# Masking the diagonal score chunks on TensorE instead of VectorE in the maximum pass of a two-pass attention kernel

## The chip, the cores and the metric

The kernel runs on one core of a Trainium2 chip. The metric is the device time of one execution in microseconds; the kernel before takes 3775.22 us (median of three runs, 3775.03 to 3777.12). TensorE (PE, with its weight loads shown apart as PEld), VectorE (DVE), ScalarE (ACT), GpSimd (POOL) and the DMA queues each have their own instruction stream, and they meet through counting semaphores.

## The reference

Input x is 2 x 2048 x 1024 in float32. One layer of causal attention with 32 query heads of 32 columns, one shared key head and one shared value head, and a bias linear in the distance; then a feed-forward layer whose low-rank part is chosen per token; a layer norm behind each. Cut to what matters here:

```python
q = (x @ Wq).reshape(b, s, 32, 32)
k, v = split(x @ Wkv)                     # one head of 32 columns each
scores = einsum('bqhd,bkd->bhqk', q, k) * scale + slopes * (kpos - qpos)
scores = where(kpos <= qpos, scores, -inf)
out = softmax(scores) @ v                 # -> @ Wo, + x, layer norm
# then: x @ W.T + b + routed low-rank part, + x, layer norm
```

## The kernel before

The attention takes the first 2870 us or so of the execution, the feed-forward part the rest; the change is in the attention alone.

**Units.** A unit `g` is one segment of 512 queries (4 tiles of 128) with 4 of the 32 heads: 2 batches x 4 segments x 8 head groups = 64 units. Segment `s` (0 to 3) of a batch sees `s + 1` segments of keys. A query's keys are handled twice: a maximum pass finds each row's largest score ahead of time, and a main pass computes the exponentials with that maximum already folded in.

**The maximum pass (step A).** For each head `h`, query tile `t` and key segment `c` there is one chunk: `scores_for_max` (L697 on) multiplies a query tile (97 rows, stationary) with 512 keys (moving) into one of three PSUM banks `ps_a` (L707), and `maximum` (L580 on) on VectorE takes the largest of each row into one column of `mxp`. In the key segment that holds the queries themselves (`c == s`), only `(t + 1) * 128` columns are needed (128, 256, 384 or 512), and the last 128 of these are a triangle that has to be masked. These masked chunks are 16 of each unit, 1024 in all; the other 1536 chunks are 512 wide and need no mask. VectorE handles an unmasked chunk with one `tensor_reduce` (L587), a masked one with `tensor_tensor_reduce` (L590), which adds the mask `maska` to the bank and takes the maximum, and which shows in the profile as two instructions: the custom operation, and a read of its accumulator into `mxp`. Before L590 VectorE's queue also holds a semaphore increment (`went_on`) that nobody waits for.

**Banks.** TensorE waits before each chunk for `a_done` of the chunk three before it (`count - 2`). VectorE waits for `a_full` of its own chunk. The transposes of x (step X) and of the maxima (step T) go through the same three banks and counters.

**The main pass (step S).** For each key tile `k` and head `h` TensorE computes scores of 128 keys by up to 512 queries into one of two banks `ps_s` (L774), adds a triangular mask on the diagonal with a second matmul of `identb` and `maskt` in bf16 (L777), and ScalarE takes the exponential into `prob` (L507). S waits for the exponential two before it (`e_done`), so no more than two score tiles stand ahead. Then `over_keys` (L719) multiplies `prob` with the values into `ps_o` and with ones into `ps_sum`: four heads side by side, each with 32 columns of weights. Each such call shows as 8 matmuls in the trace.

**What sets the order.** `plan_unit` lays steps out over the slots of a unit by tables of slot numbers: beside the S steps of unit `g` stand the A chunks of units `g + 1` and `g + 2`, the projection of the queries of unit `g + 2` (Q, L673 to L675), the transposes of x and the inversions of the row sums. All engines walk the same plan, each doing its own part, in order.

Of the kernel before, what the change touches and what calls it, by code (L numbers as in the profile page):

```python
# [6 lines left out]
ALU = mybir.AluOpType  # L7
ACT = mybir.ActivationFunctionType
AX = mybir.AxisListType
F32 = mybir.dt.float32  # L10
F32R = mybir.dt.float32r
BF16 = mybir.dt.bfloat16
I32 = mybir.dt.int32

P = 128
# [5 lines left out]
QB = 512  # L21
NSEG = T // QB
QT = QB // P
SCALE = DH ** -0.5
EPS = 1e-5
MASKED = -1.0e30
START = 1
PROBS = 6
KR = 3 * DH + 1
# [17 lines left out]
def seg_of(g):  # L47

    return g // HG
# [7 lines left out]
def full_tiles(g):  # L57

    return ktiles(g) - QT


def steps_before(g):
    return sum(ktiles(x) for x in range(g))
# [15 lines left out]
def ring(sg):  # L79

    return sg % RING * QB
# [7 lines left out]
def bank_of(count):  # L89
    return count % 3  # L90


def slot_of(count):
    return count % PROBS
# [96 lines left out]
def program(nc, x, wq, wkv, wo, w, bias, la, lb, gate_w, gate_b, out):  # L191
    nc.disable_value_cache = True
    slopes = alibi_slopes(NH)
    att = nc.dram_tensor("att_scratch", (UNITS, QT, P, P), F32, kind="Internal").ap()
    slope_rows = nc.dram_tensor("slope_rows", (NH, QB), F32, kind="Internal").ap()

    xb = x.rearrange("b (s t p) d -> (b s) p t d", t=QT, p=P)
    xt = x.rearrange("b (i p) d -> (b i) p d", p=P)
    ot = out.rearrange("b (i p) d -> (b i) p d", p=P)
    wq_v = wq.rearrange("(c p) (g m) -> g p c m", p=P, m=P)  # L200
    wo_v = wo.rearrange("(c p) n -> c p n", p=P)
    w_v = w.rearrange("(o p) n -> o p n", p=P)

    with ExitStack() as ctx:
        def sem(name):
            return ctx.enter_context(nc.semaphore(name))

        def sb(c, name, shape, dt):
            return c.enter_context(nc.sbuf_tensor(name, shape, dt))

        def pb(c, name, shape, dt=F32):
            return c.enter_context(nc.psum_tensor(name, shape, dt))

        ident = sb(ctx, "ident", [P, P], F32)
        attention(nc, sb, pb, sem, slopes, xb, wq_v, wkv, att, slope_rows, ident)
        feed_forward(nc, sb, pb, sem, xt, ot, wo_v, w_v, bias, la, lb, gate_w, gate_b, att, ident)


def attention(nc, sb, pb, sem, slopes, xb, wq_v, wkv, att, slope_rows, ident):
    with ExitStack() as ctx:  # L220
        identb = sb(ctx, "identb", [P, P], BF16)
        maska = sb(ctx, "maska", [P, QB], F32)
        maskt = sb(ctx, "maskt", [P, P], BF16)
        ones = sb(ctx, "ones", [P, DH], F32)
        slope = sb(ctx, "slope", [P, NH], F32)
# [7 lines left out]
        base = sb(ctx, "base", [GH * QT, SEGS, HG], F32)  # L233
# [11 lines left out]
        kmax = sb(ctx, "kmax", [P, RING * QB], F32R)  # L245
# [5 lines left out]
        mxp = sb(ctx, "mxp", [P, GH * QT, NSEG], F32)  # L251
# [10 lines left out]
        ps_a = [pb(ctx, f"ps_a{i}", [P, QB]) for i in range(3)]  # L262
# [6 lines left out]
        def counter(name):  # L269

            counters.append(sem(name))
            return counters[-1]

        pool_c = sem("pool_c")
# [4 lines left out]
        went_on = sem("went_on")  # L279
# [28 lines left out]
        a_done = counter("a_done")  # L308
# [5 lines left out]
        def units(prologue, unit_step, epilogue):  # L314

            prologue()  # L320
            count = FIRST
            for g in range(UNITS):
                plan = plan_unit(g)
                unit_step(g, plan, count)
                count += sum(what in ("A", "CT", "X") for what, _ in plan)
            epilogue(count)
# [3 lines left out]
        with nc.Block() as start:  # L330
            @start.sync
            def _(sp):
                for c in counters:
                    sp.sem_inc(c, START)
# [71 lines left out]
        @block.gpsimd  # L406
        def _(pool):
            nc.gpsimd.memset(ident[:], 0.0).then_inc(pool_c, 1)
            nc.gpsimd.memset(identb[:], 0.0).then_inc(pool_c, 1)
            nc.gpsimd.memset(maska[:], 0.0).then_inc(pool_c, 1)  # L410
            nc.gpsimd.memset(maskt[:], 0.0).then_inc(pool_c, 1)
            nc.gpsimd.memset(ones[:], 1.0).then_inc(pool_c, 1)
            nc.gpsimd.iota(dist_i[:], [[P, DIST0 + QT]], base=-P * DIST0, channel_multiplier=1).then_inc(pool_c, 1)
            pool.wait_ge(pool_c, 6)
            nc.gpsimd.iota(kpos_i[3 * DH:KR], [[1, QB]], base=0, channel_multiplier=0).then_inc(pool_c, 1)
            pool.wait_ge(pool_c, 7)
            for m in (ident, identb):
                nc.gpsimd.affine_select(out=m[:], in_=m[:], compare_op=ALU.not_equal, fill=1.0, base=0,
                                        pattern=[[-1, P]], channel_multiplier=1).then_inc(pool_c, 1)
            nc.gpsimd.affine_select(out=maska[:, QB - P:], in_=maska[:, QB - P:], compare_op=ALU.is_ge, fill=MASKED, base=0,  # L420
                                    pattern=[[-1, P]], channel_multiplier=1).then_inc(pool_c, 1)
            nc.gpsimd.affine_select(out=maskt[:], in_=maskt[:], compare_op=ALU.is_ge, fill=MASKED, base=0,
                                    pattern=[[1, P]], channel_multiplier=-1).then_inc(pool_c, 1)

            def split_wq(number):
                pool.wait_ge(wqh_done, START + number + 1)
                nc.gpsimd.tensor_tensor(wql[:], wq_raw[:], wqh[:].bitcast(F32), ALU.subtract).then_inc(wql_done, 1)  # L427

            def divide(g):

                pool.wait_ge(r_done, START + QT * (g + 1))
                pool.wait_ge(at_out, START + 16 * g)
                nc.gpsimd.tensor_tensor(at_sb[:], o_sb[:], r_sb[:], ALU.mult).then_inc(at_done, 1)

            def prologue():
                for number in range(3):
                    split_wq(number)

            def step(g, plan, count):
                steps = steps_before(g)  # L440
                for what, arg in plan:
                    if what == "WS":
                        split_wq(g + 3)
                    if what == "R" and arg == QT:
                        divide(g - 1)
                    if what == "ADD":
                        k = 2 * arg
                        c1 = max(0, k + 1 - full_tiles(g)) * P
                        even, odd = (prob[slot_of(steps + k + i)] for i in range(2))
                        pool.wait_ge(e_done, START + GH * (steps + k + 2))  # L450
                        pool.wait_ge(pv_done, START + steps + k + 1)
                        nc.gpsimd.tensor_tensor(even[:, :, c1:], even[:, :, c1:], odd[:, :, c1:],  # L452
                                                ALU.add).then_inc(pair_done, 1)

            units(prologue, step, lambda count: divide(UNITS - 1))
# [63 lines left out]
        def _(dve):  # L519
# [22 lines left out]
            for r in range(3):  # L542
                cols = slice(r * DH, (r + 1) * DH)
# [36 lines left out]
            def maximum(count, g, i, chunk):  # L580
                h, t, c, cols = chunk
                if i == 0:
                    dve.wait_ge(c_max, START + g)
                ps, top = ps_a[bank_of(count)][:, 0:cols], mxp[:, h * QT + t, c:c + 1]
                dve.wait_ge(a_full, START + count + 1)
                if c < seg_of(g) % NSEG:
                    nc.vector.tensor_reduce(top, ps, AX.X, ALU.max).then_inc(a_done, 1)  # L587
                else:
                    dve.sem_inc(went_on, 1)
                    nc.vector.tensor_tensor_reduce(ps, ps, maska[:, QB - cols:], 1.0, MASKED, ALU.add, ALU.max,  # L590
                                                   top).then_inc(a_done, 1)

            def reduce_max(g, count):
                s = seg_of(g) % NSEG
# [57 lines left out]
        def _(pe):  # L652
# [4 lines left out]
            for u in range(HG):  # L657
                last = nc.tensor.matmul(ps_m[0:GH * QT, P + u:P + u + 1],
                                        slope4[:, u * GH:(u + 1) * GH].rearrange("p h t -> p (h t)"),
                                        ident[:, 0:1], start=True, stop=True)  # L660
# [39 lines left out]
            def scores_for_max(count, g, i, chunk):  # L700
                h, t, c, cols = chunk
                sg = seg_of(g) // NSEG * NSEG + c
                ps, buf = ps_a[bank_of(count)], g % 3
                if i == 0:
                    pe.wait_ge(stack_in, START + 32 * (g + 1))
                pe.wait_ge(a_done, START + max(0, count - 2))
                last = nc.tensor.matmul(ps[:, 0:cols], qst[buf][0:KR, h, t * P:(t + 1) * P],  # L707
                                        kmax[0:KR, ring(sg):ring(sg) + cols], start=True, stop=True)
                last.then_inc(a_full, 1)

            def turn_max(g, count):
# [521 lines left out]
```

## Time and profile before

| | |
|---|---|
| median of three runs | 3775.22 us |
| the profiled execution | 3775.03 us |
| its span, first to last instruction | 3773.2 us |
| mean granted TensorE clock | 0.984 of full |
| busy: PE / PEld | 3582.0 us (95%) / 2207.2 us (58%) |
| busy: DVE / ACT / POOL | 2415.6 us (64%) / 1927.6 us (51%) / 1358.9 us (36%) |
| unmasked chunks on DVE (L587) | 1536, 682 ns each |
| masked chunks on DVE (L590) | 1024, 503 ns each, and 1024 accumulator reads, 130 ns each |

Matmuls are pipelined: a matmul's recorded duration is longer than the time until the next one starts, so the time that one takes on TensorE is read from start to start. A weight load (PEld) belongs to the matmul behind it and runs beside the matmul before it. A number in square brackets at the end of a row is the idle time of the engine ahead of that row and what ended it.

### The profile page before, as it was taken

The page shows a single profiled execution, that of the slowest core. Times are in us where ns is not written, and L with a number is a line of the kernel's source. Part 1 is how long each engine was busy: PE and PEld are TensorE (multiplying, and loading weights), DVE is VectorE, ACT ScalarE, POOL GpSimd, SP SyncE. Part 2 cuts the span into 40 slices and gives each one's busy share as a digit, 9 for nine tenths or more (in the row PEclk, how much of TensorE's full clock was granted, in tenths as well). Part 3 has the DMA queues.
Part 4 walks back from the last instruction along what each step waited for, and adds up shares of the span by engine and source line. Part 5 has one row for each costly group of instructions (what it writes and reads, how often), then busy time and mean ns, then how long its engine had stood idle before and what let it go on. Part 6 is the DMA issues. An engine that isn't in the chain of part 4 may idle for free. (4 is left out here: it accounts for less than half of the span.)

```text
span 3773.2 us, 56666 instructions
## 1 busy us (share of the span) xinstructions
PE 3582.0 (95%) x21057; PEld 2207.2 (58%) x21057; DVE 2415.6 (64%) x5438; ACT 1927.6 (51%) x3252; POOL 1358.9 (36%) x419
## 2 busy tenths in 40 slices
PE   5899999999999999899999999999995999999998
PEld 4555554455444444555554455544432888989987
DVE  4777777777776763777777777777742444444444
ACT  2656656666676756656666666676764101001000
POOL 1114444544455544124445554454552011011010
PEclk8999999999999999999999999999997999999999
DMA  2121110010000011111110000000003121121221
GB/s 85 46 60 32 49 32 24 24 38 23 21 15 21 15 35 32 49 57 32 49 32 24 24 15 23 21 15 21 10 7 123 45 67 55 62 67 50 67 67 40
DMA packets 157358, 148.11 MB, mean 39 GB/s; under 512 B 8356, under 2 KB 140452, under 8 KB 155016
## 3 DMA queue, kind: packets, MB, share of 16 engines
q1 hardware_dynamic: 157128, 145.07, 13.1%
q8 instruction: 140, 2.29, 0.3%
q14 instruction: 90, 0.74, 0.1%
HBM read 94.13 MB, written 33.62 MB: 34 GB/s over the span
## 5 line engine op out<-in xcount | busy, mean ns | idle before, releaser
L507 ACT ACTIVATE prob<-ps_s,alibi 128x512 f32<-128x512 f32 (+3 forms) x2560 | 1525.5, 623 | 868.6 <-PE ps_s L777 435.7
L452 POOL TENSOR_TENSOR prob<-prob 128x2048 f32<-128x2048 f32 (+1 forms) x240 | 1046.8, 4362 | 1091.4 <-ACT prob L507 1091.4
L587 DVE TENSOR_REDUCE mxp<-ps_a 128x1 f32<-128x512 f32 x1536 | 984.1, 682 | 384.4 <-PE ps_a L707 376.1
L774 PE MATMUL ps_s<-qst,kexp 97*128 97x512 f32 (+3 forms) x2560 | 1047.9, 417 | 42.5 <-ACT prob L507 28.4
L707 PE MATMUL ps_a<-kmax,qst 97*128 97x512 f32 (+3 forms) x2560 | 961.9, 396 | 38.8 <-DVE mxp L590 23.1
L774 PEld LDWEIGHTS ps_s<-qst,kexp 97*128 97x128 f32 x2560 | 481.6, 189 | 788.5 <-ACT prob L507 613.5
L719 PE MATMUL ps_o<-prob,val 128*32 128x512 f32 (+3 forms) x5120 | 602.1, 542 | 6.0 <-ACT prob L507 6.0
L590 DVE CUSTOM_DVE_ANT_0 ps_a<-ps_a,maska 128x128 f32<-128x128 f32 (+3 forms) x1024 | 495.4, 503 | 163.0 <-PE ps_a L707 130.1
L707 PEld LDWEIGHTS ps_a<-kmax,qst 97*128 97x128 f32 x2560 | 489.3, 194 | 113.4 <-DVE mxp L590 47.2
L972 POOL TENSOR_TENSOR hb_sb<-h_sb,bias_b 128x1024 f32<-128x1024 f32 x32 | 76.8, 2401 | 792.7 <-DVE z_sb L1116 732.4
L719 PE MATMUL ps_sum<-prob,ones 128*32 128x512 f32 (+3 forms) x3200 | 347.0, 513 | 0.0
L610 DVE RECIPROCAL r_sb<-s_sb 128x128 f32<-128x128 f32 x256 | 240.9, 944 | 133.0 <-ACT s_sb L513 133.0
L1002 ACT ACTIVATE root<-var 128x1 f32<-128x1 f32 x64 | 13.0, 203 | 606.5 <-DVE var L1061 606.5
L427 POOL TENSOR_TENSOR wql<-wq_raw,wqh 128x1024 fp32r<-128x1024 f32 x64 | 152.0, 2375 | 330.5 <-ACT wqh L466 330.5
L1173 PE MATMUL ps_z<-wth,hth 128*128 128x364 f32 x768 | 254.9, 332 | 5.3 <-DVE htl L1128 5.3
L1175 PE MATMUL ps_z<-wtl,hth 128*128 128x364 f32 x768 | 252.9, 329 | 0.0
L1177 PE MATMUL ps_z<-wth,htl 128*128 128x364 f32 x768 | 252.8, 329 | 0.0
L777 PE MATMUL ps_s<-maskt,identb 128*128 128x128 bf16 x1024 | 237.1, 233 | 0.0
L576 DVE SCALAR_TENSOR_TENSOR qst<-ps_m,qst 32x512 fp32r<-32x512 f32 x256 | 176.1, 688 | 80.8 <-ACT qst L473 75.6
L1165 PE MATMUL ps_y<-woh,ath 128*128 128x512 f32 x512 | 206.9, 404 | 3.9 <-DVE atl L1049 3.9
L719 PEld LDWEIGHTS ps_o<-prob,val 128*32 128x32 f32 x5120 | 105.7, 108 | 175.1 <-issue 152.5
L673 PE MATMUL ps_m<-xh,wqh 128*128 128x512 f32 x512 | 205.4, 401 | 0.4 <-DVE val L570 0.4
(147 smaller groups left out, 3673.7 us busy)
## 6 DMA issues: line engine op xcount, KB each, us to landing
wq_raw<-in_L_attn_Wq SPq DMA_DIRECT2D x64, 512.0 KB, 3.9
xs<-in_L_attn_hidden_states SPq DMA_DIRECT2D x8, 2048.0 KB, 8.1
qst<-qst SPq DMA_DIRECT2D x64, 256.0 KB
att_scratch<-at_sb SPq DMA_DIRECT2D x64, 256.0 KB, 2.4
at_raw<-att_scratch SPq DMA_DIRECT2D x32, 512.0 KB, 5.2
x_sb<-in_L_attn_hidden_states SPq DMA_DIRECT2D x32, 512.0 KB, 4.2
out<-z_sb SPq DMA_DIRECT2D x32, 512.0 KB, 3.1
z_sb<-in_L_attn_Wo SPq DMA_DIRECT2D x4, 512.0 KB, 5.4
```

What stands on the lines that cost most here:

```text
L452: nc.gpsimd.tensor_tensor(even[:, :, c1:], even[:, :, c1:], odd[:, :, c1:], ALU.add).then_inc(pair_done, 1)
L507: nc.scalar.activation(prob[slot_of(steps + k)][:, h, c0:], ps_s[h % 2][:, c0:], ACT.Exp, bias=alibi_of(g, h, k - full_tiles(g))).then_inc ...
L587: nc.vector.tensor_reduce(top, ps, AX.X, ALU.max).then_inc(a_done, 1)
L590: nc.vector.tensor_tensor_reduce(ps, ps, maska[:, QB - cols:], 1.0, MASKED, ALU.add, ALU.max, top).then_inc(a_done, 1)
L610: nc.vector.reciprocal(r_sb[:, cols], s_sb[:, cols]).then_inc(r_done, 1)
L707: last = nc.tensor.matmul(ps[:, 0:cols], qst[buf][0:KR, h, t * P:(t + 1) * P], kmax[0:KR, ring(sg):ring(sg) + cols], start=True, stop=True)
L719: last = nc.tensor.matmul(ps[h * DH:(h + 1) * DH, c0:], weights, prob[slot_of(steps_before(g) + k)][:, h, c0:], start=k == 0, stop=k == kt ...
L774: last = nc.tensor.matmul(bank[:, c0:], kexp[0:KR, at:at + P], qst[g % 3][0:KR, h, c0:], start=True, stop=not diagonal)
L777: last = nc.tensor.matmul(bank[:, c0:c0 + P], identb[:], maskt[:], start=False, stop=True)
L1173: nc.tensor.matmul(ps, hth[:, c], wth[:, c, piece(p)], start=c == 0, stop=False, skip_group_check=True)
L1175: nc.tensor.matmul(ps, hth[:, c], wtl[:, c, piece(p)], start=False, stop=False, skip_group_check=True)
L1177: last = nc.tensor.matmul(ps, htl[:, c], wth[:, c, piece(p)], start=False, stop=False, skip_group_check=True)
```

## The change

The mask goes from VectorE to TensorE, in the way that the main pass already has it. `scores_for_max` follows a masked chunk's matmul by a second one, which adds a triangle of -1e30 (`maskb`, bf16, 128 x 128) to the last 128 columns of the bank, with `identb` as its stationary operand; only this one raises `a_full`. VectorE uses the same `tensor_reduce` for every chunk, now also with 128, 256 and 384 columns; the custom operation, its accumulator read and the `went_on` increment are gone. The mask tile is smaller: 128 x 128 in bf16 instead of 128 x 512 in float32.

```diff
-        maska = sb(ctx, "maska", [P, QB], F32)
+        maskb = sb(ctx, "maskb", [P, P], BF16)
...
                 dve.wait_ge(a_full, START + count + 1)
-                if c < seg_of(g) % NSEG:
-                    nc.vector.tensor_reduce(top, ps, AX.X, ALU.max).then_inc(a_done, 1)
-                else:
-                    dve.sem_inc(went_on, 1)
-                    nc.vector.tensor_tensor_reduce(ps, ps, maska[:, QB - cols:], 1.0, MASKED, ALU.add, ALU.max,
-                                                   top).then_inc(a_done, 1)
+                nc.vector.tensor_reduce(mxp[:, h * QT + t, c:c + 1], ps_a[bank_of(count)][:, 0:cols], AX.X,
+                                        ALU.max).then_inc(a_done, 1)
...
                 last = nc.tensor.matmul(ps[:, 0:cols], qst[buf][0:KR, h, t * P:(t + 1) * P],
-                                        kmax[0:KR, ring(sg):ring(sg) + cols], start=True, stop=True)
+                                        kmax[0:KR, ring(sg):ring(sg) + cols], start=True, stop=sg < seg_of(g))
+                if sg == seg_of(g):
+                    last = nc.tensor.matmul(ps[:, cols - P:cols], identb[:], maskb[:], start=False, stop=True)
                 last.then_inc(a_full, 1)
```

On TensorE, in a unit of segment 2, one round of the four heads with masked chunks between the S steps and the products with the values. Before (`ps_a` with a number is one of the three banks, `kmax` the keys, `qst` the queries; `prob,val` are the products with the values):

```order
L774 MATMUL ps_s1<-qst1,kexp 128x512
L707 MATMUL ps_a1<-kmax,qst2 128x128
L719 MATMUL ps_o<-prob1,val 32x512 x4
L774 MATMUL ps_s0<-qst1,kexp 128x512
L707 MATMUL ps_a2<-kmax,qst2 128x256
L774 MATMUL ps_s1<-qst1,kexp 128x512
L707 MATMUL ps_a0<-kmax,qst2 128x384
L774 MATMUL ps_s0<-qst1,kexp 128x512
L707 MATMUL ps_a1<-kmax,qst2 128x512
L774 MATMUL ps_s1<-qst1,kexp 128x512
```

The same place in the changed kernel, whose lines have other numbers (L771 is S, L702 the chunk, L705 the new matmul, L716 the products):

```order
L771 MATMUL ps_s1<-qst1,kexp 128x512
L702 MATMUL ps_a1<-kmax,qst2 128x128
L705 MATMUL ps_a1<-maskb,identb 128x128
L716 MATMUL ps_o<-prob1,val 32x512 x4
L771 MATMUL ps_s0<-qst1,kexp 128x512
L702 MATMUL ps_a2<-kmax,qst2 128x256
L705 MATMUL ps_a2<-maskb,identb 128x128
L771 MATMUL ps_s1<-qst1,kexp 128x512
L702 MATMUL ps_a0<-kmax,qst2 128x384
L705 MATMUL ps_a0<-maskb,identb 128x128
L771 MATMUL ps_s0<-qst1,kexp 128x512
```

Behind every masked chunk stands one more matmul; nothing else has moved.

On VectorE, in a unit of segment 0, masked chunks between the second parts of the query split (L576). Before; each `ISA` pair is one masked chunk, the custom operation and its accumulator read:

```order
L576 SCALAR_TENSOR_TENSOR qst2<-ps_m,qst2 32x512
L590 ISA ps_a1,mxp<-ps_a1,maska 128x256
L590 ISA mxp 128x1
L590 ISA ps_a2,mxp<-ps_a2,maska 128x384
L590 ISA mxp 128x1
L576 SCALAR_TENSOR_TENSOR qst2<-ps_m,qst2 32x512
L590 ISA ps_a0,mxp<-ps_a0,maska 128x512
```

A stretch of the same kind in the changed kernel, with L585 for the chunk:

```order
L576 SCALAR_TENSOR_TENSOR qst2<-ps_m,qst2 32x512
L585 TENSOR_REDUCE mxp<-ps_a0 128x1
L585 TENSOR_REDUCE mxp<-ps_a1 128x1
L576 SCALAR_TENSOR_TENSOR qst2<-ps_m,qst2 32x512
L585 TENSOR_REDUCE mxp<-ps_a2 128x1
```

One instruction stands where two stood, in the same order.

## Rows read from the trace of the kernel before

**Rows 1.** The page, busy time of each engine
```profile
PE 3582.0 (95%) x21057; PEld 2207.2 (58%) x21057; DVE 2415.6 (64%) x5438; ACT 1927.6 (51%) x3252; POOL 1358.9 (36%) x419
```

**Rows 2.** Waits of PE: us in total, times, longest us
```profile
PE ps_s L774 <- ACT prob L507: 28.4, 88, 1.1
PE ps_a L707 <- DVE mxp L590: 23.1, 33, 1.1
```

**Rows 3.** Timeline of PE, segment 1: start us, us, engine, line, tiles
```profile
308.18 0.50 PE L774 MATMUL ps_s<-qst,kexp 97*128 97x512 f32 x1
...
308.76 0.50 PE L774 MATMUL ps_s<-qst,kexp 97*128 97x512 f32 x1
...
312.00 0.50 PE L774 MATMUL ps_s<-qst,kexp 97*128 97x512 f32 x1 [0.25 <-ACT prob L507]
312.34 0.23 PE L777 MATMUL ps_s<-maskt,identb 128*128 128x128 bf16 x1
312.38 0.48 PE L707 MATMUL ps_a<-kmax,qst 97*128 97x512 f32 x1
312.70 0.39 PE L774 MATMUL ps_s<-qst,kexp 97*128 97x512 f32 x1
```

**Rows 4.** Timeline of PE, a 128-wide chunk ahead of a projection
```profile
303.02 0.23 PE L707 MATMUL ps_a<-kmax,qst 97*128 97x128 f32 x1
303.08 0.45 PE L673 MATMUL ps_m<-xh,wqh 128*128 128x512 f32 x1
```

**Rows 5.** Timeline of PE, the existing mask matmul ahead of products with ones
```profile
1706.18 0.23 PE L777 MATMUL ps_s<-maskt,identb 128*128 128x128 bf16 x1
1706.34 1.06 PE L719 MATMUL ps_sum<-prob,ones 128*32 128x512 f32 x8
```

**Rows 6.** Timeline of PE, segment 2, one round of masked chunks
```profile
712.45 0.22 PE L707 MATMUL ps_a<-kmax,qst 97*128 97x128 f32 x1
712.60 1.06 PE L719 MATMUL ps_o<-prob,val 128*32 128x512 f32 x8
...
714.29 0.33 PE L707 MATMUL ps_a<-kmax,qst 97*128 97x384 f32 x1
714.88 0.50 PE L774 MATMUL ps_s<-qst,kexp 97*128 97x512 f32 x1 [0.26 <-ACT prob L507]
```

**Rows 7.** Timeline of ACT over the same round
```profile
714.14 1.97 ACT L507 ACTIVATE prob<-ps_s,alibi 128x512 f32<-128x512 f32 x3 [0.33 <-PE ps_s L774]
```

**Rows 8.** Groups of DVE by form: count, busy us, mean ns, idle before
```profile
L587 DVE TENSOR_REDUCE mxp<-ps_a 128x1 f32<-128x512 f32 x1536 | 984.1, 682 | 384.4 <-PE ps_a L707 376.1
...
L590 DVE CUSTOM_DVE_ANT_0 ps_a<-ps_a,maska 128x512 f32<-128x512 f32 x256 | 180.7, 706 | 26.5 <-PE ps_a L707 24.7 <-issue 0.2
...
L590 DVE CUSTOM_DVE_ANT_0 ps_a<-ps_a,maska 128x128 f32<-128x128 f32 x256 | 77.3, 302 | 56.9 <-PE ps_a L707 32.4 <-issue 23.2
```

**Rows 9.** Timeline of DVE, segment 0
```profile
102.61 0.56 DVE L590 CUSTOM_DVE_ANT_0 ps_a<-ps_a,maska 128x384 f32<-128x384 f32 x1
103.26 0.69 DVE L576 SCALAR_TENSOR_TENSOR qst<-ps_m,qst 32x512 fp32r<-32x512 f32 x1
...
104.70 0.29 DVE L590 CUSTOM_DVE_ANT_0 ps_a<-ps_a,maska 128x128 f32<-128x128 f32 x1
104.91 0.14 DVE L590 DVE_READ_ACCUMULATOR2_ANT mxp<- 128x1 f32 x1
```

**Rows 10.** Timeline of PE in the same stretch
```profile
103.46 0.36 PE L707 MATMUL ps_a<-kmax,qst 97*128 97x256 f32 x1
104.84 0.45 PE L707 MATMUL ps_a<-kmax,qst 97*128 97x384 f32 x1 [1.01 <-DVE mxp L590]
```

**Rows 11.** L590's waiters: us, times
```profile
  PEld ps_a L707: 47.2, 92
```

**Rows 12.** Timeline of PE, then of PEld, in a row of projections
```profile
1708.81 0.39 PE L674 MATMUL ps_m<-xl,wqh 128*128 128x512 f32 x1
...
1708.81 0.19 PEld L675 LDWEIGHTS ps_m<-xh,wql 128*128 128x128 f32 x1
```

More of the change, by code:

```diff
@@ L409, in _ @@
             nc.gpsimd.memset(identb[:], 0.0).then_inc(pool_c, 1)
-            nc.gpsimd.memset(maska[:], 0.0).then_inc(pool_c, 1)
+            nc.gpsimd.memset(maskb[:], 0.0).then_inc(pool_c, 1)
             nc.gpsimd.memset(maskt[:], 0.0).then_inc(pool_c, 1)
@@ L419, in _ @@
                                         pattern=[[-1, P]], channel_multiplier=1).then_inc(pool_c, 1)
-            nc.gpsimd.affine_select(out=maska[:, QB - P:], in_=maska[:, QB - P:], compare_op=ALU.is_ge, fill=MASKED, base=0,
+            nc.gpsimd.affine_select(out=maskb[:], in_=maskb[:], compare_op=ALU.is_ge, fill=MASKED, base=0,
                                     pattern=[[-1, P]], channel_multiplier=1).then_inc(pool_c, 1)
@@ L583, in maximum @@
                     dve.wait_ge(c_max, START + g)
-                ps, top = ps_a[bank_of(count)][:, 0:cols], mxp[:, h * QT + t, c:c + 1]
                 dve.wait_ge(a_full, START + count + 1)
-                if c < seg_of(g) % NSEG:
-                    nc.vector.tensor_reduce(top, ps, AX.X, ALU.max).then_inc(a_done, 1)
-                else:
-                    dve.sem_inc(went_on, 1)
-                    nc.vector.tensor_tensor_reduce(ps, ps, maska[:, QB - cols:], 1.0, MASKED, ALU.add, ALU.max,
-                                                   top).then_inc(a_done, 1)
+                nc.vector.tensor_reduce(mxp[:, h * QT + t, c:c + 1], ps_a[bank_of(count)][:, 0:cols], AX.X,
+                                        ALU.max).then_inc(a_done, 1)
             def reduce_max(g, count):
```

## The prediction

> **What bounds the kernel now.** I read the busy shares first: TensorE stands at 95%, VectorE at 64%, ScalarE at 51% [rows 1]. The waits of TensorE come next, since a share near full does not say whether it is work: TensorE records 28.4 us of idle time that the exponentials end and 23.1 us that the masked chunks' reading ends [rows 2], out of 3773. So TensorE's own queue sets the time, with two engines close enough behind it to stop it now and then. The third view is the timeline, start to start, because a matmul's recorded duration holds its pipeline's tail: a 512-wide S at 308.18 is recorded as 0.50 us, and yet a chunk and the next S both start within 0.58 [rows 3]. What the change costs is therefore the shift of the next start that an added matmul makes, and what it gives back is only what TensorE waits for VectorE. The move takes work from an engine with a third of its time free and puts it on the one that has none.
>
> **The added matmul where nothing hides it.** There are 1024 of them. The main pass already has its twin (L777: same shape, same types, its triangle added to a bank just written), so its price can be read.
>
> Ahead of a matmul with full weights: S, 512-wide chunk, S takes 308.18 to 308.76, 0.58 us; S, mask, chunk, S takes 312.00 to 312.70, 0.70 us [rows 3]. The price is 0.12 us, although the chunk starts 0.04 behind the mask (312.34 to 312.38): its record is 0.08 longer, 0.48 for 0.40, so 0.04 is the start and 0.08 an exposed rest of the weight load. Behind a 128-wide chunk part of that is paid already: the projection starts 0.06 behind such a chunk and is recorded at 0.45, 0.05 over the usual 0.40 [rows 4]. With the mask between, 0.06 + 0.04 + 0.08 = 0.18 stands where 0.06 + 0.05 = 0.11 stood: 0.07 us.
>
> Ahead of the 32-column products (L719): a 128-wide chunk is followed by them after 0.15 (712.45 to 712.60) [rows 6]. A mask is followed by them after 0.16 [rows 5] and itself starts 0.06 behind the short chunk, by rows 4: 0.22 against 0.15, again 0.07 us.
>
> What follows the 1024 masked chunks is counted in the order of the program: projections 148 (27 of them behind a 128-wide chunk), transposes of x 28, products 190, another chunk 200, an S 458.
>
> *Projections and transposes.* 121 + 28 = 149 at 0.12 and 27 at 0.07: 17.9 + 1.9 = 19.8 us. No engine is waited for here, so nothing hides it.
>
> *Products.* 190 x 0.07 = 13.3 us at most; some of these products wait for an exponential and pay nothing, so I take 11.
>
> *Another chunk.* It waits for a bank in many cases, and its price lies between 0 and 0.12. I take 0.04, the mask's own share of the starts [rows 3]: 200 x 0.04 = 8 us.
>
> *An S.* S waits for the exponential two before it. In the round of [rows 6], the S at 714.88 starts 0.59 behind the 384-wide chunk at 714.29, which itself needs some 0.18: between 0.06 for 128 columns [rows 4] and 0.24 for 512 (the 0.58 from S to S less the 0.34 that S itself takes, 312.00 to 312.34 [rows 3]). That leaves 0.4 us of room for a mask of 0.12, so its cost is 0. The S behind the 256-wide chunk may start 0.12 later, but its exponential stands in a row of three that runs without a break from 714.14 for 1.97 us [rows 7], so what is late is not waited for. Behind the 512-wide chunk the wait and the chunk end together: the mask's start of 0.04 is lost, no more. One of three loses 0.04, some S in stretches of projections lose 0.12, so the mean is between 0.01 and 0.12; I take 0.025, since rounds like this one make up the bulk: 458 x 0.025 = 11.5 us.
>
> Sum on TensorE: 19.8 + 11 + 8 + 11.5 = 50 us. Its bounds are the first two terms alone, 31 us, and 1024 x 0.12 = 123 us.
>
> In TensorE: Matmul & The Clock Gate (the Trainium skill), section Back-to-back issue gap, a stream of weight load and 128-column matmul is given at about 81 ns a pair. By that the sum would be an estimated 83 us. The trace of the twin shows 0.12 and 0.07 for the same pair, depending on what follows [rows 3 to 5], and the rows are what I use.
>
> **What VectorE gives back.** No row shows `tensor_reduce` on 128 to 384 columns. The custom operation falls from 706 ns to 302 from 512 to 128 columns, and the reduce takes 682 for 512 [rows 8]; with the same slope, 404 ns over 384 columns, the reduce is an estimated 278, 413, 548 and 682 ns. From above it can be no more than 682. The accumulator read of 0.14 looks like a pure gain and mostly is not one: the custom operation at 104.70 is followed by its read at 104.91, which is 0.09 before that operation's own recorded end [rows 9]. Where another chunk follows, the next one starts beside the read and only some 0.02 to 0.04 are gained. Where the query split follows, it has to wait for the read: 102.61 to 103.26 is 0.65 for a 384-wide chunk [rows 9], against some 0.55 to 0.58 with the reduce, so 0.1 us is gained.
>
> Is a bank free sooner? The chunk's maximum can start only when the mask is in: it is 0.06 + 0.01 later for a 128-wide chunk (0.06 to the mask's start, 0.23 of its record [rows 5] against 0.22 of the chunk's [rows 6]), and it is ready about 0.08 sooner (custom start to read end 0.21 + 0.14 = 0.35 against 0.28). So a bank comes free when it did. What TensorE gets back are the few places where VectorE is a queue behind: in the units of segment 0 it waits once for 1.01 us, at 104.84, for a backlog that began two query splits earlier [rows 9, 10], and 33 waits in all come to 23.1 us [rows 2]. There the chunks of the backlog gain 0.1 us ahead of each split and some 0.03 otherwise, 0.25 us in all, and the six masks that TensorE meets between the end of the projection and 104.84 cost nothing, since it would wait anyway, another 0.25. So half of this wait comes back, and I take the same half of all 23.1 us: 12 us.
>
> At nothing I cost the smaller mask tile and its set-up, which run in the first microseconds, ahead of the load of x that the first transposes need. The rest of the kernel, the feed-forward part included, is untouched. The removed `went_on` increment has no waiter; what it occupied on VectorE's sequencer is in the distances of [rows 9].
>
> **The sum.** 50 - 12 = +38 us. The profiled execution took 3775.0 us, 1.8 more than its span, and agrees with the median of 3775.2; so 3813 us, 1.0% slower. Its own range, with the S and chunk terms (19.5 us) between half and twice their value and the return between 5 and 25: 31 + 10 - 25 = 16 us to 31 + 39 - 5 = 65 us, 3791 to 3840.
>
> **The rivals.** *The whole price is paid.* The waits that hide masks in my sum move with TensorE itself: an S later by 0.12 makes its exponential later, and the S two behind it too, so nothing is absorbed. For it: each engine waits for the other in turn, and ScalarE idles 0.33 us ahead of the very row of three exponentials [rows 7]. Against: within that row it doesn't. Price: 149 at 0.12 and the other 875 at 0.095, halfway between 0.07 and 0.12, 18 + 83 = 101 us, and hardly any return: 3876, out of 3850 to 3898.
>
> *The weights are not hidden at all.* A matmul of full rows behind one of 97 rows would then wait for its own load. As a mechanism here: the mask's load, at half the bytes of the 0.19 us in [rows 12] an estimated 0.10, and its columns, 0.06 [rows 4], stand in the open, 0.16 us each, 164 us, 3939. Against it, L675's weights start to load at 1708.81 while L674's matmul, which starts at 1708.81, runs for 0.39 [rows 12], and both use all 128 rows. In the Trainium skill, TensorE: Matmul & The Clock Gate, section The mechanism, weight loads overlap running matmuls only if they address another group of rows; by that rule this is what would come, and the trace disagrees.
>
> *Hidden and repaid.* The S and chunk terms are zero, and VectorE's return is as large as what is left, 25 to 31 us: within 0.2% of 3775.
>
> *Faster.* VectorE, not TensorE, sets the pace where chunks come close together, in the units of segments 0 and 1. Each masked chunk leaves its queue 0.1 us sooner, the splits of the query with it, then the next chunk's bank. TensorE's 23.1 us of waits go [rows 2], and of the weight loads held up for the same reason, 47.2 us [rows 11], most too: 70 us back against 50 paid, 3755. It decides if the reduce is well below 278 ns on 128 columns, or if the backlog's start does not hang on ScalarE. Against it: with a mask ahead, a chunk's maximum starts later, and that eats the gain.
>
> **How the numbers follow.** Forecast 0.63, whole price 0.18, weights not hidden 0.02, hidden and repaid 0.10, faster 0.07. The range runs from 3772 to 3870: it holds the forecast's own range, most of the case without a change and the lower part of the whole price's, and leaves out about 0.2. Faster or slower is meant by more than 0.2%, 7.5 us, which is about what a measurement of this kernel can tell from no change. Slower 0.63 + 0.18 + 0.02 = 0.83, the same 0.10, faster 0.07.
>
> **What would show it.** In the profile after, TensorE should have 1024 more matmuls, each starting about 0.06 to 0.24 behind its chunk; the next S, chunk or projection should start 0.04 behind it with a record of 0.48, and products 0.16 behind it. The reduce should show 278, 413, 548 and 682 ns. The round of four heads in segment 2 should be about 0.11 longer (0.07 ahead of the products, 0.04 behind the 512-wide chunk) and not 0.45. The wait of 1.01 us in segment 0 should shrink to about 0.5. VectorE's busy time should fall by between 25 us (1024 times 503 against 480 on average) and, with the reads gone, 150 us and its idle time ahead of chunks should grow. I am wrong in the first step if the start behind a mask is not 0.04, in the second if the rounds grow by four times 0.1, and in the third if the waits on `mxp` vanish or grow.

## The result and the profile after

The changed kernel takes 3818.16 us (median, 3815.84 to 3820.74), against 3776.17 for the kernel before in the same comparison: a ratio of 1.0109, with a 95% interval of 1.0092 to 1.0127. It is 42 us slower (35 to 48), where 3813 and +38 were forecast. The profiled execution has a span of 3818.0 us, 44.8 more than before. Executions of one kernel differ by some 0.5%, and with it the granted clock: 3757.0 us at 0.988 and 3776.6 at 0.982 for the kernel with the mask left to four heads on VectorE.

The busy times first (the page, as in [rows 1]):

```profile
PE 3660.5 (96%) x22081; PEld 2255.5 (59%) x22081; DVE 2362.7 (62%) x4414; ACT 1929.4 (51%) x3252; POOL 1357.6 (36%) x419
```

TensorE has its 1024 matmuls more and VectorE 1024 instructions fewer. VectorE's 53 us less and TensorE's 78 us more are both poor guides to the 42: the one engine was waited for in few places, and the other's records overlap.

Where do the 42 us lie? The distance between two copies of `ps_o` into `o_sb` on ScalarE is the period of one unit. In segment 1 before and after (timeline of ScalarE, rows in between left out):

```profile
328.14 0.60 ACT L512 ACTIVATE o_sb<-ps_o 128x512 f32<-128x512 f32 x1 [1.09 <-PE ps_sum L719]
...
361.59 0.60 ACT L512 ACTIVATE o_sb<-ps_o 128x512 f32<-128x512 f32 x1 [1.09 <-PE ps_sum L719]
```
```profile
340.08 0.60 ACT L512 ACTIVATE o_sb<-ps_o 128x512 f32<-128x512 f32 x1 [1.09 <-PE ps_sum L716]
...
374.62 0.60 ACT L512 ACTIVATE o_sb<-ps_o 128x512 f32<-128x512 f32 x1 [1.09 <-PE ps_sum L716]
```

33.45 became 34.54. Read in this way for all units whose neighbours are of the same segment, most periods repeat to a few hundredths, far better than whole executions do. A few single ones do not, and they differ between executions whatever the kernel: a unit of segment 0 takes 23.3 us once in the changed kernel, and the last period takes 52.99 before, 59.73 after and 52.99 again where both engines mask. The table therefore gives medians, over 9 or 10 units of each segment, for this and for the experiments below. Every unit holds 16 masked chunks.

| kernel | segment 0 | 1 | 2 | 3 | whole, median us | ratio to before, 95% |
|---|---|---|---|---|---|---|
| before | 20.63 | 33.45 | 49.18 | 63.83 | 3776 | |
| the change | 21.43 | 34.53 | 49.63 | 64.70 | 3818.2 | 1.0109 (1.0092 to 1.0127) |
| masked on both engines | 21.71 | 34.54 | 49.61 | 64.70 | 3827.5 | 1.0137 (1.0120 to 1.0154) |
| mask matmul twice | 22.11 | 35.07 | 50.16 | 65.35 | 3853.0 | 1.0206 (1.0189 to 1.0223) |
| mask matmul 256 wide | 21.43 | 34.51 | 49.63 | 64.83 | 3819.7 | 1.0111 (1.0094 to 1.0128) |
| only 128-wide chunks on TensorE | 20.74 | 33.66 | 49.45 | 64.04 | 3782.8 | 1.0016 (1.0006 to 1.0027) |
| only 256-wide | 20.75 | 33.70 | 49.17 | 63.90 | 3784.8 | 1.0020 (1.0011 to 1.0030) |
| only 384-wide | 20.86 | 33.67 | 49.17 | 64.07 | 3788.3 | 1.0034 (1.0021 to 1.0047) |
| only 512-wide | 20.82 | 33.80 | 49.20 | 64.03 | 3790.0 | 1.0035 (1.0021 to 1.0049) |
| mask left to 4 heads, on VectorE | 20.47 | 33.44 | 49.17 | 63.81 | 3765.4 | 0.9967 (0.9953 to 0.9982) |
| mask left to 4 heads, on TensorE | 20.47 | 33.43 | 49.17 | 63.81 | 3767.4 | 0.9977 (0.9967 to 0.9986) |

The units grow by 0.80, 1.08, 0.45 and 0.87 us; the 38 units in the table hold 30 of the 42. Behind the attention nothing moves: from the last `o_sb` to the end it is 907.4 us before and 907.6 after.

The round of segment 2 that answers to [rows 6] (timeline of PE, the changed kernel; L771 is S, L702 the chunk, L705 the mask, L716 the products):

```profile
726.32 0.22 PE L702 MATMUL ps_a<-kmax,qst 97*128 97x128 f32 x1
726.38 0.23 PE L705 MATMUL ps_a<-maskb,identb 128*128 128x128 bf16 x1
726.54 1.07 PE L716 MATMUL ps_o<-prob,val 128*32 128x512 f32 x8
...
728.00 0.23 PE L705 MATMUL ps_a<-maskb,identb 128*128 128x128 bf16 x1
728.04 0.48 PE L771 MATMUL ps_s<-qst,kexp 97*128 97x512 f32 x1
728.36 0.33 PE L702 MATMUL ps_a<-kmax,qst 97*128 97x384 f32 x1
728.53 0.23 PE L705 MATMUL ps_a<-maskb,identb 128*128 128x128 bf16 x1
728.82 0.50 PE L771 MATMUL ps_s<-qst,kexp 97*128 97x512 f32 x1
729.15 0.40 PE L702 MATMUL ps_a<-kmax,qst 97*128 97x512 f32 x1
729.39 0.23 PE L705 MATMUL ps_a<-maskb,identb 128*128 128x128 bf16 x1
729.43 0.48 PE L771 MATMUL ps_s<-qst,kexp 97*128 97x512 f32 x1
729.75 0.22 PE L702 MATMUL ps_a<-kmax,qst 97*128 97x128 f32 x1
```

From the short chunk to the products it is 0.22 (726.32 to 726.54), 0.07 more. Between mask and S stand 0.04 at 728.00 and 729.39, with a record of 0.48; but 0.29 at 728.53, where S waits for its exponential: the 384-wide chunk still stands 0.46 ahead of its S. From the short chunk to the S at 728.82 it is 2.50, against 2.43 before (712.45 to 714.88) [rows 6]: of three masks only the 0.07 ahead of the products is left. The whole round, from one 128-wide chunk to the next, takes 3.43 (726.32 to 729.75), against 3.34 before, where the next one is this:

```profile
715.79 0.22 PE L707 MATMUL ps_a<-kmax,qst 97*128 97x128 f32 x1
```

Four masks cost 0.09, where 0.11 was forecast.

The hiding shows in TensorE's recorded waits for exponentials, too: 28.4 us in 88 places [rows 2] have become 17.0 in 47 (waits of PE, the changed kernel):

```profile
PE ps_s L771 <- ACT prob L507: 17.0, 47, 1.1
```

And the reductions (groups of DVE by form, to be held against [rows 8]):

```profile
L585 DVE TENSOR_REDUCE mxp<-ps_a 128x1 f32<-128x512 f32 x1792 | 1157.8, 681 | 415.1 <-PE ps_a L702 377.9 <-PE ps_a L705 26.6
...
L585 DVE TENSOR_REDUCE mxp<-ps_a 128x1 f32<-128x384 f32 x256 | 141.6, 553 | 57.1 <-PE ps_a L705 51.2
L585 DVE TENSOR_REDUCE mxp<-ps_a 128x1 f32<-128x256 f32 x256 | 107.9, 422 | 63.2 <-PE ps_a L705 59.7
L585 DVE TENSOR_REDUCE mxp<-ps_a 128x1 f32<-128x128 f32 x256 | 72.4, 283 | 63.7 <-PE ps_a L705 62.0
```

283, 422, 553 and 681 ns, where 278, 413, 548 and 682 had been estimated from the slope.

### The profile page after: what moved, and what is told of

It reads as the page before. It is cut to its first block and busy times, and to the rows that moved or that the text cites. A ratio compares the mean times of both kernels' runs of the same rounds, so it can differ in the third digit from the quotient of the medians.

```text
span 3818.0 us, 56682 instructions
## 1 busy us (share of the span) xinstructions
PE 3660.5 (96%) x22081; PEld 2255.5 (59%) x22081; DVE 2362.7 (62%) x4414; ACT 1929.4 (51%) x3252; POOL 1357.6 (36%) x419
## 5 line engine op out<-in xcount | busy, mean ns | idle before, releaser
L585 DVE TENSOR_REDUCE mxp<-ps_a 128x1 f32<-128x512 f32 (+3 forms) x2560 | 1449.2, 603 | 599.0 <-PE ps_a L702 377.9
L771 PE MATMUL ps_s<-qst,kexp 97*128 97x512 f32 (+3 forms) x2560 | 1071.5, 424 | 34.9 <-ACT prob L507 17.0
L702 PE MATMUL ps_a<-kmax,qst 97*128 97x512 f32 (+3 forms) x2560 | 969.8, 397 | 21.0 <-DVE mxp L585 8.8
L771 PEld LDWEIGHTS ps_s<-qst,kexp 97*128 97x128 f32 x2560 | 486.6, 191 | 728.1 <-ACT prob L507 523.3
L716 PE MATMUL ps_o<-prob,val 128*32 128x512 f32 (+3 forms) x5120 | 603.2, 543 | 6.0 <-ACT prob L507 6.0
L702 PEld LDWEIGHTS ps_a<-kmax,qst 97*128 97x128 f32 x2560 | 497.0, 195 | 70.6 <-DVE mxp L585 23.9
L716 PE MATMUL ps_sum<-prob,ones 128*32 128x512 f32 (+3 forms) x3200 | 344.6, 510 | 0.0
L576 DVE SCALAR_TENSOR_TENSOR qst<-ps_m,qst 32x512 fp32r<-32x512 f32 x256 | 176.2, 688 | 115.0 <-ACT qst L473 109.7
L705 PE MATMUL ps_a<-maskb,identb 128*128 128x128 bf16 x1024 | 237.1, 232 | 0.0
L668 PE MATMUL ps_m<-xh,wqh 128*128 128x512 f32 x512 | 217.3, 425 | 0.4 <-DVE val L570 0.4
L670 PE MATMUL ps_m<-xh,wql 128*128 128x512 f32 x512 | 204.0, 399 | 0.0
```

The lines of the kernel that those rows point to most:

```text
L585: nc.vector.tensor_reduce(mxp[:, h * QT + t, c:c + 1], ps_a[bank_of(count)][:, 0:cols], AX.X, ALU.max).then_inc(a_done, 1)
L705: last = nc.tensor.matmul(ps[:, cols - P:cols], identb[:], maskb[:], start=False, stop=True)
L716: last = nc.tensor.matmul(ps[h * DH:(h + 1) * DH, c0:], weights, prob[slot_of(steps_before(g) + k)][:, h, c0:], start=k == 0, stop=k == kt ...
L771: last = nc.tensor.matmul(bank[:, c0:], kexp[0:KR, at:at + P], qst[g % 3][0:KR, h, c0:], start=True, stop=not diagonal)
```

## The experiments

### The price on TensorE by itself: both engines mask

```diff
+                if c < seg_of(g) % NSEG:
                     nc.vector.tensor_reduce(...)
+                else:
+                    nc.vector.tensor_tensor_reduce(..., maska[:, QB - cols:], 1.0, MASKED, ALU.add, ALU.max, ...)
```

The changed kernel with the old reduction of masked chunks put back.

> The masked chunks get the new mask matmul on TensorE, and VectorE keeps its old masking reduction too (the mask is added twice, which changes nothing in the maximum). So the whole price on TensorE is paid and nothing is given back by VectorE. The forecast's account (price about 50 us of which the rest is hidden in waits for the exponentials, return about 12): 3776 + 50 to 60 = 3826 to 3836. The rival account of the same +42 (whole price of about 100 us paid, 57 us of it returned by VectorE): 3876. In the units of segment 0, 20.6 us each before and 21.4 after, the forecast expects 21.4 to 21.9, the rival 22.4.

Measured: 3827.5 us, +52 (1.0137, 45 to 58 us). So the price on TensorE is 52 us, and the change's own +42 leaves about 10 us for VectorE's return. The rival account of 100 paid and 57 returned is out. In segment 0 the unit takes 21.71, inside the forecast's span and far from 22.4. In segments 1 to 3 the units are the same as in the changed kernel, to 0.02 us: in an ordinary unit there the cheaper reduction is worth nothing.

### VectorE's return by itself: the mask left to four heads

```diff
-                if c < seg_of(g) % NSEG:
+                if c < seg_of(g) % NSEG or g % HG:
                     nc.vector.tensor_reduce(...)
```

No mask matmul. The maximum is only a shift, so a bound above it serves as well, as long as the exponentials stay in range. The bias grows with the slope of the head to about 0.84 x 127 = 107 over a triangle in the first head, which I took to be too much, and from the fifth head on to at most 53. The first four heads keep their mask; no run tried them without it.

> No mask matmul; VectorE uses the plain reduction on all chunks except those of the first four heads, which keep the old masking one (for the other 28 heads the maximum may be taken over the triangle too, since it only has to be a bound that the exponentials survive). 896 of 1024 chunks thus show VectorE's return alone, and without the 0.07 us by which a mask matmul delays each reduction. The forecast: 10 to 15 us, 3761 to 3766. The rival with a large return: 50 us, 3726. A third view, that VectorE's time is worth nothing here because TensorE sets the pace: 3776.

Measured: 3765.4 us, -11 (0.9967, 0.9953 to 0.9982, which is 7 to 18 us). The return is small and real, and of the size that the forecast had. The units show where: 20.63 to 20.47 in segment 0 and nothing in the other ordinary units; more comes in the units that also prepare the next segment (the fifth one of segment 0 goes from 34.1 to 33.2). One place is the wait of [rows 10]. In this kernel (timeline of PE; L708 is the chunk):

```profile
106.28 0.36 PE L708 MATMUL ps_a<-kmax,qst 97*128 97x256 f32 x1
107.36 0.45 PE L708 MATMUL ps_a<-kmax,qst 97*128 97x384 f32 x1 [0.71 <-DVE mxp L586]
```

1.38 us between these two chunks have become 1.08: VectorE's backlog is 0.30 shorter, of which the unit keeps 0.16. With both engines masking (L712 the chunk, L715 the mask) it is 0.88, because the masks ahead of it have made TensorE later against a backlog that did not move:

```profile
111.17 0.36 PE L712 MATMUL ps_a<-kmax,qst 97*128 97x256 f32 x1
111.38 0.23 PE L715 MATMUL ps_a<-maskb,identb 128*128 128x128 bf16 x1
112.05 0.44 PE L712 MATMUL ps_a<-kmax,qst 97*128 97x384 f32 x1 [0.44 <-DVE mxp L594]
```

and in the changed kernel the two together leave 0.58, with no idle time recorded on TensorE. The wait has not gone altogether, for the chunk's weight load still waited 0.28 us for the reduction, against 0.57 with both engines masking (timeline of PE and PEld):

```profile
109.66 0.36 PE L702 MATMUL ps_a<-kmax,qst 97*128 97x256 f32 x1
109.86 0.23 PE L705 MATMUL ps_a<-maskb,identb 128*128 128x128 bf16 x1
110.23 0.19 PEld L702 LDWEIGHTS ps_a<-kmax,qst 97*128 97x128 f32 x1 [0.28 <-DVE mxp L585]
110.24 0.44 PE L702 MATMUL ps_a<-kmax,qst 97*128 97x384 f32 x1
```

### The same with the four heads masked on TensorE

```diff
-                if sg == seg_of(g):
+                if sg == seg_of(g) and g % HG == 0:
                     last = nc.tensor.matmul(ps[:, cols - P:cols], identb[:], maskb[:], start=False, stop=True)
```

> As the one before, but the first four heads' chunks are masked by the new matmul on TensorE instead (128 mask matmuls, no custom operation anywhere). The forecast prices 128 of them at 0.05 us, 6 us, and gives 1 to 2 us back: 3 to 6 us above the kernel with the first four heads masked on VectorE, so 3765 to 3771. The whole-price rival puts 128 x 0.10 = 13 us on it: 13 above.

Measured: 3767.4 us (0.9977, 0.9967 to 0.9986), 2 us above the one before, and their intervals overlap: 128 masks are too few to tell 3 from 6 us. The 13 us of the rival would have shown, if narrowly. Both kernels still compute the layer of the reference, and both are faster than the two that this study began with: by 0.2 to 0.3% than the kernel before.

### The price twice

```diff
+                    last = nc.tensor.matmul(ps[:, cols - P:cols], identb[:], maskb[:], start=False, stop=False)
                     last = nc.tensor.matmul(ps[:, cols - P:cols], identb[:], maskb[:], start=False, stop=True)
```

> The mask matmul is issued twice behind each masked chunk (the same stationary operand and the same triangle). The second one starts behind a 128-column matmul whose own load is not hidden. If what hides a mask is the wait of the next S for its exponential, about half of the second one is hidden too: the forecast expects 0.06 to 0.10 us where nothing waits and 45 to 60 us more in all, 3863 to 3878. If nothing is hidden and the price is the same everywhere, 1024 x 0.10 = 100 us more, 3920.

Measured: 3853.0 us, 35 more than the change, where 45 to 60 were expected: it is cheaper than either account had it. The trace bears on why (timeline of PE; L705 and L706 are the two masks):

```profile
739.06 0.23 PE L705 MATMUL ps_a<-maskb,identb 128*128 128x128 bf16 x1
739.13 0.22 PE L706 MATMUL ps_a<-maskb,identb 128*128 128x128 bf16 x1
739.16 0.48 PE L772 MATMUL ps_s<-qst,kexp 97*128 97x512 f32 x1
```

The second mask starts 0.07 behind the first and S 0.03 behind the second, still with 0.48: S is 0.06 later than with one mask (0.10 against 0.04). As I read it, the first mask pays a whole 0.12 since it also pulls S's weight load into the open, and the second finds it there already. The units grow by 0.68, 0.54, 0.53 and 0.65 for 16 more masks, 0.03 to 0.04 each, where 0.06 is the open price: about half is hidden, as was said. Of the open price that was forecast for it, 0.06 to 0.10, the second mask pays the least.

### What is paid: the load or the columns

```diff
-                    last = nc.tensor.matmul(ps[:, cols - P:cols], identb[:], maskb[:], start=False, stop=True)
+                    wide = min(cols, 2 * P)
+                    last = nc.tensor.matmul(ps[:, cols - wide:cols], identb[:], maskb[:, 2 * P - wide:], start=False,
+                                            stop=True)
```

> The mask matmul moves 256 columns instead of 128 behind the 768 chunks that are 256 columns or wider (zeros and the triangle). Steps read the price of the mask as 0.04 us of start and 0.08 us of a weight load that shows, behind 128 moving columns. If the exposed load is what is paid, 128 more columns hide it: where a full-weight matmul follows, the next start moves from 0.04 to about 0.10 and its record shrinks from 0.48 to 0.42 or less, and the kernel stays within 10 us of the changed kernel, 3818 to 3828. If the columns are what is paid, each wide mask costs 0.05 to 0.06 more wherever nothing waits: 768 x 0.055 x one half to all = 21 to 42 us more, 3839 to 3860.

Measured: 3819.7 us (1.0111), the same as the changed kernel's 1.0109. 128 columns more in 768 matmuls cost nothing that the whole time can show. The units agree to 0.02 in segments 0 to 2; segment 3 takes 0.13 more. Nor is it a wait that hides the columns: ahead of projections, where nothing waits, S to S with a 256-wide chunk takes 1.17 (timeline of PE, segment 1; L706 the wide mask, L773 S, L668 the projection), against 1.18 with the narrow mask and 1.06 with none:

```profile
313.05 0.40 PE L773 MATMUL ps_s<-qst,kexp 97*128 97x512 f32 x1
...
313.40 0.28 PE L706 MATMUL ps_a<-maskb,identb 128*128 128x256 bf16 x1
313.44 0.48 PE L668 MATMUL ps_m<-xh,wqh 128*128 128x512 f32 x1
...
314.22 0.39 PE L773 MATMUL ps_s<-qst,kexp 97*128 97x512 f32 x1
```

So up to 256 columns it is not the columns that set the price, and the next instruction's load is what fits: a matmul ahead of full weights takes some 0.12 whether it has 128 columns or 256, and 0.06 ahead of a second mask. That the load is the cause is argued from these distances; no run changed the load alone. The detail of the expectation was wrong, though. What follows the wide mask does not start later and its record does not shrink: 0.04 (313.40 to 313.44) and 0.48, as with the narrow mask, and it is the same where an S follows (726.06 and 726.10 in this kernel). A recorded start is thus no measure of what was paid; only the distance over two or three matmuls is safe to read.

### Width by width

```diff
-                if sg == seg_of(g):
+                if sg == seg_of(g) and t == 2:
```

Four kernels, each with only one width of masked chunk (`t` = 0 to 3) on TensorE with the plain reduction, the other three masked on VectorE as before.

> Only the 256 chunks that are 128 wide get the mask matmul and the plain reduction. By the forecast's steps: 58 at 0.04, 104 ahead of products at 0.07, 27 ahead of a projection at 0.07, 65 ahead of an S at 0.025 and 2 at 0.12: 2.3 + 7.3 + 1.9 + 1.6 + 0.2 = 13 us, less about 3, +10: 3786. The 0.07 ahead of products is not absorbed by any wait, so the round of segment 2, whose period is set by the way from the last S through the products, should grow by 0.07, and a unit of segment 2 (49.2 us) by about 0.3.

> Only the 256 chunks that are 256 wide get the mask matmul and the plain reduction. By the forecast's steps: 46 ahead of a chunk at 0.04, 18 ahead of products at 0.07, 69 ahead of projections and transposes at 0.12, 123 ahead of an S at 0.025: 1.8 + 1.3 + 8.3 + 3.1 = 14.5 us, less 3 returned by VectorE, +11.5, so 3788. It completes a test of whether the price is a sum over masks: the four widths alone should add up to the whole, +42 us; 384 and 128 alone gave +12 and +6.5, so 256 and 512 together should give about 23. If masks hide each other's cost in a shared wait, the four add up to less than the whole; if each alone leaves VectorE's gain unused, to more.

> Only the 256 chunks that are 384 wide get the mask matmul and the plain reduction; all others keep the masking reduction on VectorE. By the forecast's steps: 76 at 0.04, 44 at 0.07, 21 at 0.12 and 115 ahead of an S at 0, since that S waits 0.4 us for an exponential: 3.0 + 3.1 + 2.5 = 9 us, less about 3 returned, +6, so 3782. If all widths cost the same, a quarter of +42: +10.5, 3786. In the round of segment 2 the S behind the 384-wide chunk should start as far behind it as before (0.59 us).

> Only the 256 masked chunks that are 512 wide get the mask matmul and the plain reduction. By the forecast's steps: 20 at 0.04, 24 at 0.07, 57 at 0.12, 155 ahead of an S at 0.025: 0.8 + 1.7 + 6.8 + 3.9 = 13.2 us, less 3, +10, so 3786. In the round of segment 2 the S behind the 512-wide chunk should be 0.04 later.

Measured, by the ratios: 6 us for 128 (2 to 10), 8 for 256 (4 to 11), 13 for 384 (8 to 18), 13 for 512 (8 to 19). They were expected at 10, 11.5, 6 and 10: the first two are cheaper, the last two dearer, and only the 10 of the 128-wide and of the 512-wide chunks lie within the measured intervals. The four add up to 40, against 42 for the change, with intervals too wide to tell a sum from less than one. The units say it more finely, and there the four add up to less than the whole in every segment: 0.65 against 0.80 in segment 0, 1.03 against 1.08, 0.27 against 0.45, and 0.72 against 0.87. That is the sign that the expectation gave for masks which hide in a shared wait. In segment 2 only the 128-wide chunks cost anything alone (+0.27, as forecast: four rounds of 0.07), 256 and 384 nothing and 512 0.02. The S behind the 512-wide chunk does start 0.04 behind the mask, as expected (timeline of PE, 512-wide alone):

```profile
718.88 0.40 PE L712 MATMUL ps_a<-kmax,qst 97*128 97x512 f32 x1
719.12 0.23 PE L715 MATMUL ps_a<-maskb,identb 128*128 128x128 bf16 x1
719.16 0.48 PE L781 MATMUL ps_s<-qst,kexp 97*128 97x512 f32 x1
719.47 0.22 PE L712 MATMUL ps_a<-kmax,qst 97*128 97x128 f32 x1
```

But from this chunk to the next it is 0.59, where it was 0.57 before (715.22 to 715.79): the 0.04 of the recorded start is not what is paid. The S there was recorded at 0.50 already without a mask. In the round of the 384-wide kernel (timeline of PE) the S behind the mask starts 0.59 behind its chunk, as in [rows 6]:

```profile
714.54 0.33 PE L712 MATMUL ps_a<-kmax,qst 97*128 97x384 f32 x1
714.72 0.23 PE L715 MATMUL ps_a<-maskb,identb 128*128 128x128 bf16 x1
715.13 0.50 PE L781 MATMUL ps_s<-qst,kexp 97*128 97x512 f32 x1 [0.18 <-ACT prob L511]
```

In segments 0, 1 and 3, 384-wide chunks cost 0.23, 0.22 and 0.24 for four masks, 0.06 each. There the forecast's zero for the S does not hold, and +6 was short of the +13 (8 to 18).

## Why the prediction was right

**What bounds the kernel** was right: the time follows TensorE's starts. VectorE's relief alone gives 11 us (7 to 18), and nothing in the ordinary units of three segments of four.

**The price in the open** was right to a hundredth. Ahead of projections (timeline of PE, segment 1, the changed kernel):

```profile
313.97 0.50 PE L771 MATMUL ps_s<-qst,kexp 97*128 97x512 f32 x1
314.30 0.22 PE L702 MATMUL ps_a<-kmax,qst 97*128 97x128 f32 x1
314.37 0.23 PE L705 MATMUL ps_a<-maskb,identb 128*128 128x128 bf16 x1
314.41 0.48 PE L668 MATMUL ps_m<-xh,wqh 128*128 128x512 f32 x1
...
315.18 0.40 PE L771 MATMUL ps_s<-qst,kexp 97*128 97x512 f32 x1
...
316.36 0.39 PE L771 MATMUL ps_s<-qst,kexp 97*128 97x512 f32 x1
```

S to S is 1.21 with a 128-wide chunk and 1.18 with a 256-wide one. The same two stretches before (the chunk of [rows 4] lies in the first) took 1.14 and 1.06: 0.07 and 0.12.

```profile
302.68 0.50 PE L774 MATMUL ps_s<-qst,kexp 97*128 97x512 f32 x1
...
303.82 0.40 PE L774 MATMUL ps_s<-qst,kexp 97*128 97x512 f32 x1
...
304.88 0.40 PE L774 MATMUL ps_s<-qst,kexp 97*128 97x512 f32 x1
```

**The sum on TensorE**, 50 us, is measured at 52 (45 to 58). The units show which term was off. By the forecast's own prices and the order of the program, an ordinary unit should grow by 0.93, 0.98, 0.63 and 0.64 us in segments 0 to 3. The kernel that masks on both engines, which pays and gets next to nothing back, grows by 1.08, 1.09, 0.43 and 0.87. The first two are near. In segment 2, five products at 0.07 leave 0.08 us for 11 S, 0.01 each; in segment 3, the same five and one other chunk at 0.04 leave 0.48 for 10 S, 0.05 each. The forecast took 0.025 for every S, mostly from the round of [rows 6], which turned out the cheapest place, and that the mean fits is in part luck.

**VectorE's return**, 12 us, is measured at 10 to 11. The estimates of the reduction's duration were good to 9 ns. The waits that it was worked out from did not go as described, and here, too, the number is in part luck. In its place the wait was to shrink to half, and more of it went: the two chunks stand 0.58 apart instead of 1.38, through a backlog 0.30 shorter and masks of 0.50 ahead of it. Elsewhere half was too generous. TensorE's recorded waits for `mxp` were 26.7 us (23.1 for masked chunks [rows 2] and 3.6 for the others); with both engines masking they are 14.5 (11.3 and 3.2), and in the changed kernel 8.8 (waits of PE; L594 is the masked reduction of the kernel that masks on both):

```profile
PE ps_a L712 <- DVE mxp L594: 11.3, 22, 0.9
```
```profile
PE ps_a L702 <- DVE mxp L585: 8.8, 16, 1.1
```

So 12 of the 18 us were taken up by the masks themselves, which made TensorE arrive later, and some 6 by the relief. A second wait on VectorE is not in the forecast at all. The transpose of the maxima waits for `mx`, the last reduction of a unit: 0.60 us in each of eleven units, nearly all of segment 0, and 0.35 where both engines mask (one wait of 3.8 us, ahead of the first unit, is in every kernel):

```profile
PE ps_a L714 <- DVE mx L596: 10.4, 12, 3.8
```
```profile
PE ps_a L721 <- DVE mx L601: 7.6, 12, 3.8
```

In the changed kernel, and where the mask is left to four heads, those eleven are no longer recorded. How much of the 10 us each of the two waits gave back was not separated.

**The rivals.** The whole price of 101 us is refuted by the kernel that masks on both engines, 58 us at most. Hidden and repaid, within 0.2% of the time before, is refuted by the +42 (35 to 48), and its return of 25 to 31 us by the kernel with the mask left to four heads on VectorE, 18 at most for seven eighths of the chunks. The same kernel refutes faster by VectorE's relief, which needed 70. That weights are not hidden at all would have cost 164. For the mask's own load that is refuted by 52. A part of it fits what was measured here: behind a matmul of only 128 columns, which take 0.06, the next full load seems to show, since the price is 0.12.

## What to carry to other kernels

Price an added matmul by what follows it: here its own 128 columns were about half of the 0.12 us in the open (a second mask cost 0.06), and the rest went, as far as the distances tell, to the weight load of the next instruction, no longer covered. Then price each kind of place by itself, for one round does not stand for all: an S behind a mask came to 0.01 us in segment 2 and 0.05 in segment 3. Work moved to the engine that has no slack is paid in full wherever that engine does not wait, and what it frees on the other engine is worth at most the waits that ended there: here 10 us, while its busy time fell by 53. And ask first whether the work is needed at all: a maximum that serves only as a shift needs no exact mask, and leaving it out for 28 of 32 heads gave the only two versions faster than both.

## What the runs showed of the hardware that was not expected

- A mask of 256 columns in place of 128 cost nothing ahead of a projection or an S, with the same starts and records around it (0.04 and 0.48); only the units of segment 3 grew, by 0.13.
- A second mask behind the first cost 0.06 in the open, half of what the first cost.
- Putting 1024 custom operations and accumulator reads back moved the ordinary units of segments 1 to 3 by 0.02 us or less. That tells how much room VectorE has there, not what a read costs.
- A recorded start can move by 0.04 with nothing paid: the S behind the mask of a 512-wide chunk.
